# A fused attention, mixture-of-experts and layer norm kernel: the last two row tiles finished one at a time on VectorE

## The reference, cut to what matters

```python
x = layernorm(x + attention(x, ...))      # 4096 rows of 512, window attention, 8 heads
x = layernorm(x + ffn(x, ...))            # the part that the change touches

def ffn(x):
    scores = softmax(x @ gate_w.T)        # 8 experts
    weights, idx = top_k(scores, 2)
    y = sum over the 2 chosen experts of weight * (silu(x @ w1.T) * (x @ w3.T)) @ w2.T
    z = silu(x @ ws1.T) * (x @ ws3.T) @ ws2.T      # the shared expert, for every row
    return y + z

def layernorm(x):                         # no scale, no shift, eps = 1e-5
    return (x - mean(x)) / sqrt(var(x) + eps)
```

## Time and profile before

| | |
|---|---|
| median of 3 runs | 1669.78 us (1668.85 to 1669.81) |
| the profiled execution's own time | 1665.29 us |
| its span in the trace | 1663.6 us |
| TensorE busy | 1615.4 us (97% of the span) |
| VectorE busy | 830.0 us (50%) |
| ScalarE busy | 655.6 us (39%) |
| GpSimd busy | 708.7 us (43%) |

### The profile page before, as it was taken

The page is one execution under the profiler, slowest core; times in us unless marked ns, Lnnn a source line. Parts: engine busy times, 40 slices in busy tenths (PEclk is TensorE's granted clock), DMA queues, the critical chain, the costliest instruction groups (busy, mean ns, idle before and its releaser), DMA issues.

```text
span 1663.6 us, 31095 instructions
## 1 busy us (share of the span) xinstructions
PE 1615.4 (97%) x9466; PEld 1348.3 (81%) x9467; DVE 830.0 (50%) x2303; ACT 655.6 (39%) x1564; POOL 708.7 (43%) x774
## 2 busy tenths in 40 slices
PE   7999999999999999999999999988999999999997
PEld 6888998899889988998899889865677777777774
DVE  5555556655655566556556665566222222222365
ACT  4334334433443344334433443354233333333355
POOL 3323333333343243333432433422555555555465
PEclk9999999999999999999999999998999999999999
DMA  8021101111111111111111111359355556556696
GB/s 288 32 75 46 33 33 51 44 32 32 50 44 32 32 51 44 32 32 53 42 32 32 55 40 32 92 148 277 87 102 101 101 102 102 102 103 127 189 314 232
DMA packets 83916, 143.19 MB, mean 86 GB/s; under 512 B 10664, under 2 KB 27560, under 8 KB 83328
## 3 DMA queue, kind: packets, MB, share of 16 engines
q1 hardware_dynamic: 59792, 95.96, 17.5%
q0 software_dynamic: 18304, 38.24, 13.2%
q10 hardware_dynamic: 5776, 8.43, 1.9%
HBM read 94.75 MB, written 56.76 MB: 91 GB/s over the span
## 4 chain that ended last, share of the span: by engine, by line
PE 56%; issue 26%; POOL 7%; DVE 5%; DMA 3%; ACT 1%; SPq 1%; POOLq 0%; ACTq 0%; DVEq 0%
PE bank L1078 16%; PE bank L1153 15%; PE bank L1105 10%; PE bank L1228 6%; POOL rnorm L670 4%; PE bank L1052 3%; PE bank L1247 2%; POOL slot_d L655 2%; PE bank L1215 1%; PE bank L1088 1%; DVE qkn L1401 1%; POOL pp L676 1%; DMA bx<-x_d 1%; DMA passing<-in_wqkvT 1%; PE bank L1202 1%
## 5 line engine op out<-in xcount | busy, mean ns | idle before, releaser
L1153 PE MATMUL bank<-wh,xh 128*128 128x512 f32 (+2 forms) x896 | 338.5, 378 | 4.7 <-DVE wl L1357 2.0
L1153 PE MATMUL bank<-wl,xh 128*128 128x512 f32 (+2 forms) x896 | 327.6, 366 | 0.0
L1153 PE MATMUL bank<-wh,xl 128*128 128x512 f32 (+2 forms) x896 | 326.8, 365 | 0.0
L670 POOL TENSOR_TENSOR rnorm<-ssmax,nhalf 128x4 f32<-128x4 f32 x128 | 132.0, 1031 | 403.6 <-DVE ssmax L1393 398.4
L1153 PEld LDWEIGHTS bank<-wh,xh 128*128 128x128 f32 x896 | 169.8, 190 | 36.4 <-DVE qkn L1401 9.9
L1153 PEld LDWEIGHTS bank<-wh,xl 128*128 128x128 f32 x896 | 169.9, 190 | 28.5
L1153 PEld LDWEIGHTS bank<-wl,xh 128*128 128x128 f32 x896 | 170.0, 190 | 22.6
L1379 DVE TENSOR_TENSOR bl<-bank,bh 128x512 fp32r<-128x512 f32 x104 | 71.7, 690 | 179.8 <-ACT bh L832 179.5
L758 POOL DMA_INDIRECT eo_d<-eo,dstc x72 | 115.4, 1603 | 101.0 <-ACT eo L1017 77.1
L1401 DVE TENSOR_TENSOR qkn<-bank,rnorm 128x512 f32<-128x512 f32 x128 | 88.6, 692 | 131.3 <-POOL rnorm L670 131.3
L1247 PE MATMUL bank<-woh,oh 128*128 128x256 f32 (+1 forms) x512 | 147.5, 288 | 1.0 <-DVE xr L1466 1.0
(11 more groups left out here) (202 smaller groups left out, 3496.7 us busy)
## 6 DMA issues: line engine op xcount, KB each, us to landing
eo_d<-zero_d SPq DMA_DIRECT2D x34, 256.0 KB, 3.0
xt<-in_xT SPq DMA_DIRECT2D x33, 256.0 KB, 3.2
xr<-in_x SPq DMA_DIRECT2D x32, 256.0 KB, 2.7
x_d<-xr SPq DMA_DIRECT2D x32, 256.0 KB, 2.1
eo_d<-xr SPq DMA_DIRECT2D x32, 256.0 KB, 2.3
bx<-x_d SPq DMA_DIRECT2D x32, 256.0 KB, 7.4
ga<-eo_d SPq DMA_DIRECT2D x16, 512.0 KB, 5.5
gb<-eo_d SPq DMA_DIRECT2D x16, 512.0 KB, 7.8
```

Of the source, the lines that this page charges most:

```text
L670: pool.tensor_tensor(rnorm[:, :], ssmax[:, :], nhalf[:, :], ALU.pow).then_inc(rn_s, 1)
L1153: mm = pe.matmul(b[:, 0:n], a[:, par, c, :], wt[:, c, cols], start=(c == 0 and k == 0), stop=(c == DC - 1 and k == 2))
```

## The change

The last pair is no longer taken as a pair. ScalarE's copies of the last two output products into `zs` go, and so do its normalisation of the last pair and GpSimd's `pair_power` for it. Instead VectorE finishes each of the two tiles in `finish_tile(k)`: it adds `ga` to the product straight from its bank, takes the statistics, adds eps, waits for GpSimd to raise that one column to -1/2 (`tile_power`), and subtracts the mean and multiplies by the result in one instruction (`tensor_scalar` with two per-row scalars). Tile 0 comes in step `q` = 103, behind `gate_hidden(103)`, tile 1 in the step after it. SyncE's last two stores wait for the new semaphore `last_s` instead of `o_s`.

```diff
@@ sync: store_pair
-                    sp.wait_ge(o_s, 2 * n + k + 1)
+                    sp.wait_ge(*((last_s, k + 1) if n == LAST else (o_s, 2 * n + k + 1)))
@@ gpsimd
+            def tile_power(k):
+                r = rs2[:, LAST % 2, k:k + 1]
+                pool.wait_ge(fve, 2 * LAST + k + 1)
+                pool.tensor_tensor(r, r, nhalf[:, 0:1], ALU.pow).then_inc(frs, 1)
...
-                    pair_power(n)
+                    if n < LAST:
+                        pair_power(n)
+                if q0 >= NQ - 1:
+                    tile_power(q0 - NQ + 1)
@@ scalar
-                if 1 <= n <= PAIRS:
+                if 1 <= n <= LAST:
                     normalise(n - 1)
...
-                if q0 - 1 >= FIRST:
+                if FIRST <= q0 - 1 < NQ - 2:
@@ vector
+            def finish_tile(k):
+                z, b = z_of(LAST)[:, k, :], LAST % 2
+                dve.wait_ge(gab_s, LAST + 1)
+                dve.wait_ge(eo_s, NQ - 1 + k)
+                dve.tensor_tensor(z, bank[6 + (NQ + k) % 2][:, :], ga[:, LAST % 4, k, :], ALU.add).then_inc(y_s, 1)
+                dve.wait_ge(y_s, lates(LAST) + k)
+                if k == 0:
+                    dve.wait_ge(fnm, LAST)
+                m = 2 * LAST + k
+                dve.wait_ge(fmv, m)
+                dve.bn_stats(bn6[:, :], z).then_inc(fbn, 1)
+                dve.wait_ge(fbn, m + 1)
+                dve.bn_aggr(mv2[:, b, k, :], bn6[:, :]).then_inc(fmv, 1)
+                dve.wait_ge(fmv, m + 1)
+                dve.tensor_scalar(rs2[:, b, k:k + 1], mv2[:, b, k, 1:2], EPS, None, ALU.add).then_inc(fve, 1)
+                dve.wait_ge(frs, LAST + 1 + k)
+                if k == 0:
+                    dve.wait_ge(o_out[b], 32 * (LAST // 2))
+                dve.tensor_scalar(oo[:, b, k, :], z, mv2[:, b, k, 0:1], rs2[:, b, k:k + 1], ALU.subtract, ALU.mult)\
+                   .then_inc(last_s, 1)
...
-                if n < PAIRS:
+                if n < LAST:
                     total(n)
...
+                if q0 >= NQ - 1:
+                    finish_tile(q0 - NQ + 1)
```

More of the change, by code:

```diff
@@ L317, in block_kernel @@
         y_s = sem("y_s")
+        last_s = sem("last_s")
         fbn = sem("fbn")
@@ L420, in block_kernel @@
         SLOT_Q = S1 - 3
+        LAST = PAIRS - 1
         EARLY = S1 // 2
```

## The result

| | before | after |
|---|---|---|
| median of 22 runs each, in turn on the same chips | 1667.98 us (1664.80 to 1669.88) | 1664.38 us (1661.62 to 1667.88) |
| ratio after / before, 95% interval | | 0.9981 (0.9975 to 0.9987) |
| the profiled execution's own time, and its span | 1665.29, 1663.6 us | 1665.58, 1663.8 us |
| last product's end to the last store's issue | 7.12 us | 3.78 us |

The 7.12 us take the product's length from the timeline (1.98); the prediction's 7.10 has the chain's 2.00.

The account below looks back on a forecast made before the run. TensorE bounds nearly the whole run, but behind its last product a single line of waits sets the end. Its new terms move the last issue from 1661.07 to 1657.78: 1669.78 - 3.3 = 1666.5 us, range 1665.2 to 1668.2.

Parts of the forecast that it names:

- The tail's new chain: After the last product, VectorE finishes both tiles in line; last store issued at about 1657.78 in place of 1661.07.
- Tile 0's wait for `fnm` = 15: Tile 0's statistics on VectorE wait for GpSimd's last pair 14 instruction, until 1652.41; costs tile 0 0.79 us.
- A trip to GpSimd and back: Per last tile, VectorE's wait for GpSimd's power of one column: 0.71 us, 0.86 with eps.
- the lone last store: Last store goes out alone; its 2.53 us to the end kept, though nothing to 0.3 us may come off.
- the -3.3 us: Predicted saving in the tail behind the last product, from the last store's issue moving from 1661.07 to 1657.78.
- the edge of 0.2%: Whole kernel: about 0.2% (3.3 us) can be told from no change; faster beyond it 0.50, within 0.46, slower 0.04.
- Rival 1: Tail: tile 0 does not stand in tile 1's way; -4.0 us, 1665.8 us in the median; chance 0.10.
- Rival 2: Tail: two trips to GpSimd in line are dear, 2 x 0.44 us more; -2.4 us, 1667.4 us; chance 0.10.
- Rival 3: Kernel's end: something unseen behind the stores sets it, so the time stays at 1669.8 us; chance 0.06.
- rival 4: Tail: slower once a trip costs more than 2.5 us; at 2.9 us +0.8, 1670.6 us; chance 0.04.
- The last product still ends about 1653.97: Sign in the changed profile: TensorE's last product is unmoved; if moved, something ahead changed and the base is off.
- How the numbers follow: Step from tail to total: 3.3 us off the profiled 1665.29 and the median 1669.78, giving 1666.5 us; forecast's chance 0.70.

Follow-up runs that it names:

- own counts: Changed kernel with two new semaphores for tiles 30 and 31, so tile 0's statistics need not wait for pair 14; 8.32 us from sum 14's end to last issue, for 8.93.
- interleaved: Changed kernel with VectorE taking both last tiles' sums, statistics and eps first, then both normalisations; 8.57 us from sum 14's end to last store issue, for 8.93.

## Why the prediction was right in the difference and wrong in the time

**The tail's new chain: right.** Between the last product and the last issue I had 1657.78 - 1653.97 = 3.81 us. Two traces of the change show 3.78 and 3.79; the second has 3.44, because there tile 1's sum was only 0.38 us late to its product. Tile 0's wait for `fnm` = 15, 0.79 us by my sum, was 0.86 in the first trace; the run with its own counts shows that it decides. A trip to GpSimd and back is 0.66 or 0.67 us for my 0.71, each normalisation 0.55 for 0.54, a sum from the bank 0.68 for 0.69, and the lone last store changed nothing at the end. Tile 1 came 0.72 us late to its product in the first trace, where I had 0.70. So the -3.3 us were right by their terms. The 0.19% lies just inside the edge of 0.2%, for which I had 0.46, against 0.50 beyond it.

**Rival 1** (tile 0 not in the way) is what the run "own counts" is, by edit: 0.6 us, which I had at 0.66. The change itself does not do it. **Rival 2** (dear trips) is refuted: no trip was longer than 0.67 us in any trace of the change. Where a normalisation runs beside a power, as in the interleaved runs, the power rises from 0.55 to 0.81; that is the only price of this kind seen here, and after's order avoids it. **Rival 3** (no difference) and **rival 4** (slower) are refuted by the interval.

**What I had left out of the rivals.** "The last product still ends about 1653.97" was not so: it ended at 1657.56, and I had said that this would mean that my base is off. It is VectorE's sum of pair 14 that comes before the last gate. Its length was 1.23 to 3.35 us over 14 traces, by when GpSimd adds pair 15's halves, and it is the same code in both kernels. I had weighed such meetings of the two engines for the new instructions only, and taken all ahead of them as fixed. So a moved last product was no sign of changed code. From the start of the last hidden product to the last issue before took 15.31, 16.22 (with the slow product taken out) and 15.40 us, after 12.90, 11.57 and 11.68: the sum moves single executions by about 1 us, in either kernel. In the profiled pair the sum cost after 0.92 us, and the last hidden product started 2.7 us later (1.6 of it at the low clock around 1086 us). That hides the 3.3 us: 2.68 + 0.92 - 3.33 = 0.27 us, and the spans differ by 0.2, since the end came 0.07 us sooner behind the last issue (2.46 for 2.53 us).

**The step that failed is "How the numbers follow": its base.** I took "the same microseconds off the median: 1669.78 - 3.3" and gave the range "0.6 for what two programs differ by". The 3 runs of that median spanned 1 us, but the profiled execution beside them was 4.5 us shorter, and that was the sign that one execution differs from another by more. Over 22 runs before spans 5.1 us, with its median at 1667.98: the base was 1.8 us too high. The three runs shown are among the seven highest of the 22. 1667.98 - 3.3 = 1664.7 would have been 0.3 us from the measured time. The range of +-1.5 us held the uncertainty of the sum, and nothing for that of the base.

What stays open is why TensorE's clock is low around 1086 us in one execution and not in another, and whether the order of a few instructions 570 us later can bear on it (one of three traces of before, ten of eleven of the others). If it can, the changed kernels lose on average 1.6 x (10/11 - 1/3) = 0.9 us that stand beside the tail's 3.3, by an estimate from those counts; the measured 2.2 to 4.2 us allow it either way. Open too is why the way from the slot table to the first gather was once 16.7 us.

## What to carry to other kernels

In a tail, write down who comes last at each meeting of two engines, and what is next when it goes: here the wait taken away gave 0.6 us, and then TensorE was next; the product brought forward by 1.4 us gave nothing, because VectorE was already the later one. Work that is moved off the last item (tile 0 done while TensorE makes tile 1) pays, and shorter instructions for it gave nothing here, undone one at a time. Where single executions scatter by 5 us, compare stretches between two named instructions, which agreed to 0.02 us where the engines met in the same order, check that order first (10.03 against 8.93 us), and give a range for the total that holds the scatter of the base.

## What the runs showed of the hardware

- Two two-input sums over 128x1024, one on VectorE and one on GpSimd, do not share time. VectorE's sum, 1.23 us alone, ended 1.07 to 1.09 us behind the end of GpSimd's in all eleven traces in which GpSimd's had started first, and took 1.89 to 3.35 us. The other way round a 128x2 product on GpSimd took 1.27 us in place of 0.20, up to the end of VectorE's sum.
- With 2.50 us of idle time ahead of it TensorE went on at full clock in some executions of before (a 128x512 matmul 0.39 us, one start every 0.23) and at 1.2 GHz in another (0.63 us, one every 0.43, for more than half of twelve), at the same place of the same program. In the first trace of after and in own counts the first two to four matmuls behind the idle time were still at full clock, and the low clock came behind them.
- Small waits across engines were alike in the traces of the change: 0.03 us from GpSimd's power to VectorE's normalisation, 0.08 or 0.09 us from GpSimd's `nm` to VectorE's statistics, 0.08 or 0.09 us from VectorE's eps to GpSimd's power, 0.02 us from VectorE's end to SyncE's issue.
